# Second chunk's gathers of angles on two semaphores, each waiting for the landing of the one two places ahead

## The chip, the cores and the metric

The kernel runs on one core of a Trainium2 chip. The core has five engines with instruction streams of their own: TensorE (PE in the profile), VectorE (DVE), ScalarE (ACT), GpSimd (POOL) and SyncE (SP). They meet through semaphores, and they share 16 DMA engines. The metric is the device time of one launch in microseconds; the runs of the kernel before took 378.64, 381.76 and 385.66 us, median 381.76.

## The reference, cut to what matters

4,096 token ids (8 batches of 512) each pick a row of 36 angles out of a table of 8,000 rows. The angles drive a simulated circuit of six qubits; its six expectation values, times a matrix and plus a bias, are the embedding of 192 features. A layer norm and an attention over the 512 tokens of a batch follow, then another layer norm and a mixture of eight experts of which each token uses two.

```python
params = quantum_params[token_ids.reshape(-1)]        # 4096 rows of 36 angles
ev = _circuit_expvals(params)                         # sin and cos of half angles, 6 numbers per token
emb = ev @ post_w.T + post_b
h = emb
h = h + attention(layernorm(h))                       # 8 batches of 512 tokens
h = h + top2_of_8_experts(layernorm(h))
```

## The kernel before, in words

Tokens are laid out 128 to a tile, one per partition, so there are 32 tiles of four to a batch. The circuit is computed for two chunks of 16 tiles each (`CHUNK_BATCHES = (4, 4)`). Everything here happens in the first fifth of the run.

**POOL** (`gpsimd` block) sets up an identity, waits for the token ids and then issues 32 indirect DMAs, one per tile, each gathering 128 rows of 36 angles from DRAM into `theta_all` (`gather_angles`, line 421). Each adds 16 to a semaphore when it has landed: the first 16 to that of chunk 0, the others to that of chunk 1. None of them waits for another. Behind them on the same engine stand `constants` (lines 556 to 571), the reciprocal root of chunk 0's variance (`rstd1`, line 540), the pair strings of the second chunk's circuit (`pair_strings(1)`), and later the scatters of rows to experts (line 551) and the final scatter-adds into the output (line 593).

**DVE** (`vector` block) works through a list written out by hand: preparations of weights; `reduce_angles(0)` (lines 655 to 665), which waits until all of chunk 0's angles have landed; copies of weight products; the circuit of chunk 0 in the parts `rotations` (682 to 690), `matrices` (720 to 750), `strings`, `pairs`, `sums`; then `reduce_angles(1)` with its wait for chunk 1's angles; the rest of chunk 0's circuit (`expectations`) and its weights and variance; then the circuit of chunk 1, whose pairs are on POOL. ACT takes sine and cosine of each chunk as soon as the angles are reduced. The attention of chunk 0's batches starts once DVE has written `w` (line 1038), at which PE's transposes (line 1470) wait. Instructions of one part of the circuit stand on DVE in order; `cjoin` waits for those before.

SP loads the small weights and the experts' up weights at the start; the padding of the routing table and the down weights come only when DVE has finished chunk 0's circuit.

Of the kernel before, what the change touches and what calls it, by code (L numbers as in the profile page):

```python
# [30 lines left out]
def build(nc, token_ids, angles, emb_two, emb_raw, qkv_w, gate_w, up_w, down_w, out):  # L31
# [16 lines left out]
    STEPS = -(-BLOCKS // STEP)  # L48
    ROWS = E * REGION + 2 * STEP * P
    RING = 4  # L50
    RESULTS = 8
    CHUNKS = len(CHUNK_BATCHES)
    LAST = [sum(CHUNK_BATCHES[:c + 1]) for c in range(CHUNKS)]
    TILE0 = [(LAST[c] - CHUNK_BATCHES[c]) * TILES for c in range(CHUNKS)]
# [18 lines left out]
    with ctx:  # L73
# [3 lines left out]
        def sem(name):  # L77
            return ctx.enter_context(nc.semaphore(name))
# [88 lines left out]
        def behind(room, pattern, **sizes):  # L167
            size = int(np.prod(list(sizes.values())))
            room[1] += size
            return room[0][:, room[1] - size:room[1]].rearrange(pattern, **sizes)  # L170
# [54 lines left out]

        xb = behind(up_room_1, "p (r n f) -> p r n f", r=RING, n=STEP, f=F)
        y = behind(up_room_1, "p (n d) -> p n d", n=RESULTS, d=D)
        t_own = behind(up_room_1, "p (m x) -> p m x", m=BLOCKS, x=1)
# [8 lines left out]
        bank_d = ctx.enter_context(nc.psum_tensor("bank_d", [P, 512], F32))  # L237

        ids_in = sem("ids_in")
        angles_in = [sem(f"angles_in{c}") for c in range(CHUNKS)]  # L240
        small_in = sem("small_in")
        up_in = sem("up_in")
        down_in = sem("down_in")
# [73 lines left out]
        order_done = sem("order_done")  # L317
        block_in = [sem(f"block_in{r}") for r in range(RING)]
        pick_done = sem("pick_done")
# [7 lines left out]
        y_done = sem("y_done")  # L327
        added = [sem(f"added{n}") for n in range(RESULTS)]
        landed = sem("landed")
# [28 lines left out]
        def _(sp):  # L358
# [23 lines left out]
            def load_block(m):  # L382
                row = sp.value_load(t_i[0:1, 0, m:m + 1], min_val=0, max_val=ROWS - P)
                sp.dma_start(xb[:, m // STEP % RING, m % STEP, :], routed[bass.ds(row, P), :]
                             ).then_inc(block_in[m // STEP % RING], 16)

            sp.sem_inc(landed, 1)
            sp.wait_ge(scattered, 16 * 2 * T)
            sp.wait_ge(table_done, 1)
            for m in range(RING * STEP):  # L390
                if m >= STEP or m % 2 == 0:
                    load_block(m)
            for m in range(BLOCKS):
                sp.wait_ge(added[m % RESULTS], 16 * (m // RESULTS) + 16)
                sp.sem_inc(landed, 1)
                if m + RING * STEP < BLOCKS:
                    load_block(m + RING * STEP)
# [3 lines left out]
        def _(pool):  # L401
# [15 lines left out]
            def gather_angles(first, last):  # L417
                for t in range(first, last):
                    b, j = divmod(t, TILES)
                    c = [b < n for n in LAST].index(True)  # L420
                    pool.indirect_dma_start(out=theta_all[:, t, :], out_offset=None, in_=angles,  # L421
                                            in_offset=bass.IndirectOffsetOnAxis(ids[:, b, j:j + 1], 0)
                                            ).then_inc(angles_in[c], 16)

            step(pool.memset(minus_half[:, :], -0.5))
            pool.wait_ge(ids_in, 16)
            gather_angles(0, T)

            psteps = [0]
# [158 lines left out]
            for m in range(BLOCKS):  # L588
# [6 lines left out]
                        xb[:, m // STEP % RING, m % STEP, DEST:DEST + 1].bitcast(I32), 0),  # L595
                    in_=y[:, m % RESULTS, :], in_offset=None, bounds_check=TOKENS - 1,
                    oob_is_err=False, compute_op=ALU.add).then_inc(added[m % RESULTS], 16)

        @block.vector
        def _(dve):  # L600
# [41 lines left out]
            def cstep(instruction):  # L642
                csteps[0] += 1
                instruction.then_inc(circuit_step, 1)

            def cjoin():
                dve.wait_ge(circuit_step, csteps[0])

            def reduce_angles(c):

                n = COUNT[c]
                theta = theta_all[:, TILE0[c]:TILE0[c] + n, 0:USED]
                count, near, fold = [a[:, 0:n, 0:USED] for a in (turns, turned, folded)]
                dve.wait_ge(angles_in[c], 16 * n)
                cstep(dve.tensor_scalar(count, theta, 1 / (2 * math.pi), ROUNDER, ALU.mult, ALU.add))
                cjoin()
                cstep(dve.tensor_scalar(count, count, ROUNDER, None, ALU.subtract))
                cjoin()
                cstep(dve.scalar_tensor_tensor(theta, count, -TWO_PI_HIGH, theta, ALU.mult, ALU.add))
                cjoin()  # L660
                cstep(dve.scalar_tensor_tensor(theta, count, -TWO_PI_LOW, theta, ALU.mult, ALU.add))
                cjoin()
                dve.tensor_scalar(near, theta, PI_BELOW, -PI_BELOW, ALU.min, ALU.max).then_inc(reduced, 1)  # L663
                dve.wait_ge(reduced, c + 1)
                dve.scalar_tensor_tensor(fold, near, -1.0, near, ALU.mult, ALU.max).then_inc(folded_done, 1)
# [273 lines left out]
            def both_ends(c):  # L939
# [41 lines left out]
            dve.tensor_tensor(form_d[0:E, 0, :, :], bank_b[0:E, 0, 0:E].unsqueeze(2).to_broadcast([E, E, E]), delta,  # L981
                              ALU.mult).then_inc(score_spread, 1)
            reduce_angles(0)
            dve.wait_ge(m2t_done, 1)

# [140 lines left out]
            for part in circuit_parts[0:5]:  # L1126
                part(0)
            reduce_angles(1)
            expectations(0)
            weights()  # L1130
# [51 lines left out]
            c = 0  # L1182
            for shift in (1, 2, 4):
# [3 lines left out]
                c = 1 - c  # L1187
# [57 lines left out]
            def weighted(m):  # L1245
                dve.wait_ge(y_mm, m + 1)
                if m >= RESULTS:
                    dve.wait_ge(added[m % RESULTS], 16 * (m // RESULTS))
# [462 lines left out]
```

## Time and profile before

| what | value |
|---|---|
| runs | 378.64, 381.76, 385.66 us; median 381.76 |
| the profiled execution | 382.33 us, of which the span from first to last instruction is 380.6 |
| busy time over the span | PE 234.4, DVE 171.6, ACT 94.3, POOL 244.9 us |
| gathers of angles (line 421) | 32, from 3.4 to 44.9 us of the span, 32.1 us busy |
| DMA traffic while they run alone | a tenth of the 16 engines' time |

The profile gives for each engine its instructions with start and duration from the span's start, the idle time before them and what seems to have ended it. "issue" is idle time for which the profile shows no releaser. For an indirect DMA the row has the time that POOL worked on issuing it, not the transfer; transfers show in the DMA rows.

### The profile page before, as it was taken

How to read it: one execution, taken by the hardware profiler on the slowest of the kernel's cores; microseconds unless marked ns; L12 is line 12 of the kernel's file. 1: busy time of each engine (PE TensorE's matmuls, PEld its weight loads, DVE VectorE, ACT ScalarE, POOL GpSimd, SP SyncE). 2: the span in 40 equal slices, each digit the busy share in tenths (PEclk: the TensorE clock that was granted, in tenths of full speed). 3: DMA queues.
4: the chain of work that ended last, by engine and by line, in shares of the span. 5: the costliest groups of instructions: out<-in, count | busy, mean ns of one | idle time of the engine just before them, and what ended most of it. 6: DMA issues, size and time to landing. Idle time of an engine off the chain costs nothing. (4 is left out here: it accounts for less than half of the span.)

```text
span 380.6 us, 6129 instructions
## 1 busy us (share of the span) xinstructions
PE 234.4 (62%) x1590; PEld 158.5 (42%) x1590; DVE 171.6 (45%) x649; ACT 94.3 (25%) x221; POOL 244.9 (64%) x259
## 2 busy tenths in 40 slices
PE   1724930067744867673462438999999948999700
PEld 0513510023422434442231215777777726777500
DVE  5836299987466675553153274232232111322200
ACT  1002002015331344440321312342424312333100
POOL 6777700499332657777367751888888388888864
PEclk9999985555685796766555558999999996999955
DMA  7510100890000010110111111655555255555520
GB/s 217 134 16 13 14 1 0 344 373 2 0 0 2 12 52 10 55 51 13 48 48 54 59 47 20 65 65 63 63 62 58 26 58 62 63 65 58 55 27 0
DMA packets 28141, 22.61 MB, mean 59 GB/s; under 512 B 15434, under 2 KB 25546, under 8 KB 27787
## 3 DMA queue, kind: packets, MB, share of 16 engines
q0 software_dynamic: 13296, 7.95, 18.7%
q1 hardware_dynamic: 14524, 14.23, 11.7%
q8 instruction: 15, 0.25, 0.3%
q14 instruction: 18, 0.15, 0.1%
q10 hardware_dynamic: 288, 0.03, 0.1%
HBM read 7.25 MB, written 15.63 MB: 60 GB/s over the span
## 5 line engine op out<-in xcount | busy, mean ns | idle before, releaser
L593 POOL DMA_INDIRECT out<-up x71 | 110.3, 1554 | 40.8 <-DVE up L1249 15.7
L1640 PE MATMUL bank_b<-down,up 128*128 x426 | 87.5, 342 | 5.2 <-issue 1.5
L551 POOL DMA_INDIRECT routed<-rows,slot x64 | 62.3, 973 | 37.0 <-issue 23.1
L1640 PEld LDWEIGHTS bank_b<-down,up 128*128 128x128 f32 x426 | 69.5, 192 | 22.9 <-issue 18.9
L1249 DVE TENSOR_SCALAR up<-bank_b,up 128x192 f32<-128x192 f32 x71 | 29.7, 418 | 96.7 <-PE bank_b L1640 69.2
L421 POOL DMA_INDIRECT theta_all<-angles,ids x32 | 32.1, 1003 | 11.1 <-issue 9.4
L1381 ACT ACTIVATE up<-bank_a 128x384 f32<-128x384 f32 x71 | 31.3, 497 | 2.8 <-PE bank_a L1630 2.4
L540 POOL TENSOR_TENSOR rs<-ve,minus_half 128x16 f32<-128x16 f32 x2 | 7.4, 3711 | 36.8 <-DVE ve L1026 36.8
L1497 PE MATMUL bank_b<-queries_t,keys_t 32*128 32x512 f32 x64 | 24.3, 841 | 7.9 <-DVE nmax L1043 3.0
L1504 PE MATMUL bank_a<-keys_t,wt 32*128 32x512 f32 x64 | 26.1, 898 | 3.4 <-ACT keys_t L1276 2.0
L1570 PE MATMUL bank_a<-m,a2t 32*128 32x192 f32 x64 | 13.6, 510 | 22.7 <-ACT hres L1306 12.1
L1043 DVE TENSOR_REDUCE nmax<-bank_a 128x2 f32<-128x1024 f32 x16 | 19.5, 1219 | 16.3 <-PE bank_a L1504 16.3
L1393 ACT COPY up<-bank_c 128x384 f32<-128x384 f32 x18 | 8.6, 478 | 63.0 <-PE bank_c L1619 50.7
L1470 PE MATMUL bank_a<-ident,w 128*128 128x128 f32 x8 | 3.1, 388 | 31.2 <-DVE w L1038 27.0
L1619 PE MATMUL bank_c<-up_all,up 128*128 128x384 f32 x36 | 16.3, 536 | 9.7 <-DVE up L1209 9.0
L1298 ACT ACTIVATE prob<-bank_b 128x1024 f32<-128x1024 f32 x16 | 16.4, 1023 | 20.1 <-PE bank_b L1497 18.9
L1570 PEld LDWEIGHTS bank_a<-m,a2t 32*128 32x128 f32 x64 | 7.1, 260 | 29.7 <-issue 23.1
L1630 PE MATMUL bank_a<-up 32*128 32x128 f32 x426 | 17.8, 295 | 0.4 <-ACT up L1387 0.4
L1264 ACT ACTIVATE sine<-angle_stages 128x480 f32<-128x480 f32 x2 | 2.1, 1063 | 60.3 <-DVE angle_stages L663 60.3
L1630 PEld LDWEIGHTS bank_a<-up 32*128 32x128 f32 x426 | 14.5, 193 | 4.9 <-issue 4.4
L1470 PEld LDWEIGHTS bank_a<-ident,w 128*128 128x128 f32 x8 | 1.5, 184 | 35.1 <-issue 35.1
L1516 PE MATMUL bank_c<-prob,u 128*32 128x128 f32 x256 | 13.7, 376 | 1.3 <-ACT prob L1298 1.0
(396 smaller groups left out, 373.5 us busy)
## 6 DMA issues: line engine op xcount, KB each, us to landing
routed<-pad_rows SPq DMA_DIRECT2D x8, 528.0 KB, 5.0
out<-hres SPq DMA_DIRECT2D x8, 384.0 KB
down<-down_w SPq DMA_DIRECT2D x1, 2304.0 KB, 9.7
up<-up_w SPq DMA_DIRECT2D x1, 1536.0 KB
out<-up POOLq DMA_INDIRECT x71, 3.5
up<-routed SPq DMA_DIRECT2D x69, 16.0 KB
routed<-rows,slot POOLq DMA_INDIRECT x64
up<-up_w SPq DMA_DIRECT2D x1, 780.0 KB
```

The lines of the kernel that those rows point to most:

```text
L421: pool.indirect_dma_start(out=theta_all[:, t, :], out_offset=None, in_=angles, in_offset=bass.IndirectOffsetOnAxis(ids[:, b, j:j + 1], 0)) ...
L551: pool.indirect_dma_start(out=routed, out_offset=bass.IndirectOffsetOnAxis(slot[:, b, k, j:j + 1], 0), in_=rows[:, b, k, j, :], in_offset= ...
L593: pool.indirect_dma_start(out=out_rows, out_offset=bass.IndirectOffsetOnAxis(xb[:, m // STEP % RING, m % STEP, DEST:DEST + 1].bitcast(I32) ...
L1043: dve.tensor_reduce(nmax[:, b % 2, 2 * h:2 * h + 2], bank_a[:, 0:2, :], AX.X, ALU.max, negate=True).then_inc(max_done, 1)
L1249: dve.tensor_scalar(y[:, m % RESULTS, :], bank_b[:, m % 2, 0:D], xb[:, m // STEP % RING, m % STEP, SHARE:SHARE + 1], None, ALU.mult).then_ ...
L1298: act.activation(prob[:, 2 * h:2 * h + 2, :], bank_b[:, :, :], ACT.Exp).then_inc(exp_done, 1)
L1381: act.activation(hid[:, n, :], bank_a[:, n, 0:HID], ACT.Gelu).then_inc(gelu_done, 1)
L1497: mm = pe.matmul(bank_b[:, n, :], keys_t[r, bt % 3, k * P:(k + 1) * P], queries_t[r, :], start=True, stop=True)
L1504: mm = pe.matmul(bank_a[:, n, :], wt[r, bs % 2, :], keys_t[r, bs % 3, :], start=True, stop=True)
L1570: mm = pe.matmul(bank_a[:, 2 + n, 0:D], a2t[r, :], m2[r, :], start=True, stop=True)
L1630: mm = pe.matmul(bank_a[:, n, c * P:(c + 1) * P], up_now[r, s % 2, c * P:(c + 1) * P], xt[r, 0, :], start=True, stop=True)
L1640: mm = pe.matmul(bank_b[:, m % 2, 0:D], hid[:, m % STEP, c * P:(c + 1) * P], down[:, bass.ds(first + c * D, D)], start=(c == 0), stop=(c = ...
```

## The change

A constant `IN_FLIGHT = 2` is added. Each chunk gets two semaphores in place of one, and its gathers add to them in turn. In the second chunk (c > 0), a gather from the third on first waits until its semaphore has 16 for each earlier gather of the same turn, that is, until the gather two places ahead has landed: 14 waits in all. The first chunk's 16 gathers still wait for nothing. `reduce_angles` waits for both semaphores of its chunk, 128 each, where it waited for one at 256.

```diff
+    IN_FLIGHT = 2
...
-        angles_in = [sem(f"angles_in{c}") for c in range(CHUNKS)]
+        angles_in = [[sem(f"angles_in{c}_{i}") for i in range(IN_FLIGHT)] for c in range(CHUNKS)]
...
                     c = [b < n for n in LAST].index(True)
+                    turn_of, k = divmod(t - TILE0[c], IN_FLIGHT)
+                    if c > 0 and turn_of > 0:
+                        pool.wait_ge(angles_in[c][k], 16 * turn_of)
                     pool.indirect_dma_start(out=theta_all[:, t, :], out_offset=None, in_=angles,
                                             in_offset=bass.IndirectOffsetOnAxis(ids[:, b, j:j + 1], 0)
-                                            ).then_inc(angles_in[c], 16)
+                                            ).then_inc(angles_in[c][k], 16)
...
-                dve.wait_ge(angles_in[c], 16 * n)
+                for k in range(IN_FLIGHT):
+                    dve.wait_ge(angles_in[c][k], 16 * n // IN_FLIGHT)
```

## Rows read from the trace of the kernel before

**Rows 1.** Page, part 1: busy us (share of the span) and instructions of each engine

```profile
PE 234.4 (62%) x1590; PEld 158.5 (42%) x1590; DVE 171.6 (45%) x649; ACT 94.3 (25%) x221; POOL 244.9 (64%) x259
```

**Rows 2.** Timeline of DVE: start us, us, line, operation, tiles, shape [idle before]

```profile
35.05 0.25 DVE L690 TENSOR_TENSOR turn<-cosine,sine 128x96 f32<-128x96 f32 x1
36.57 0.42 DVE L720 TENSOR_TENSOR step_m<-cosine,bloch 128x256 f32<-128x256 f32 x1 [1.27 <-DVE turn L690]
...
37.94 0.19 DVE L733 TENSOR_TENSOR parity<-bloch 128x32 f32<-128x32 f32 x1
38.64 0.17 DVE L734 COPY parity<-bloch 128x16 f32<-128x16 f32 x1 [0.51 <-issue]
...
47.74 0.20 DVE L743 COPY pair_e<-bloch 128x64 f32<-128x64 f32 x1 [1.06 <-issue]
48.45 0.31 DVE L744 TENSOR_TENSOR last_r<-turn 128x144 f32<-128x144 f32 x1 [0.52 <-issue]
48.68 0.18 DVE L747 TENSOR_TENSOR last<-turn,bloch 128x32 f32<-128x32 f32 x1
...
61.94 0.40 DVE L655 TENSOR_SCALAR angle_stages<-theta_all 128x480 f32<-128x480 f32 x1
```

**Rows 3.** Those who stand still until DVE is done, POOL and PE timelines

```profile
71.35 3.71 POOL L540 TENSOR_TENSOR rs<-ve,minus_half 128x16 f32<-128x16 f32 x1 [24.75 <-DVE ve L1026]
77.74 0.45 PE L1470 MATMUL bank_a<-ident,w 128*128 128x128 f32 x1 [26.98 <-DVE w L1038]
```

**Rows 4.** Windows: stretch, us, busy PE, PEld, DVE, ACT, POOL, clock, DMA, GB/s

```profile
36.50:38.00 1.50, 1.50 (x4) 0.97 (x4) 1.43 (x8) 0.00 (x0) 1.20 (x2) 1.00 0.08 12
38.00:48.40 10.40, 10.40 (x25) 5.66 (x24) 2.23 (x11) 0.00 (x0) 7.00 (x15) 1.00 0.10 13
48.40:61.90 13.50, 2.36 (x8) 1.07 (x6) 13.13 (x70) 0.00 (x0) 0.00 (x0) 0.70 0.00 0
```

**Rows 5.** Timeline of POOL, gathers of angles and what follows them

```profile
3.38 1.18 POOL L421 DMA_INDIRECT theta_all<-angles,ids  x1 [1.67 <-DMA ids<-token_ids]
...
34.24 1.89 POOL L421 DMA_INDIRECT theta_all<-angles,ids  x1 [0.30 <-issue]
...
42.72 0.95 POOL L421 DMA_INDIRECT theta_all<-angles,ids  x1 [0.30 <-issue]
43.98 0.95 POOL L421 DMA_INDIRECT theta_all<-angles,ids  x1 [0.30 <-issue]
44.94 0.22 POOL L556 IOTA blk_i<- 128x71 int32 x1
...
46.32 0.28 POOL L569 CAST before<-before_f 128x128 bf16<-128x128 f32 x1
```

**Rows 6.** DMA, 43.98 to 47.98 us in 40 slices of 0.1 us: busy tenths, GB/s

```profile
DMA  0000630000000000552000000000000000000000
GB/s 0 0 0 12 92 69 0 12 0 0 0 0 0 0 0 0 69 81 35 0 0 0 0 0 0 0 0 0 0 0 0 0 0 0 0 0 0 0 0 0
```

**Rows 7.** Timeline of SP and page, part 6: the load of the ids, last number to landing

```profile
0.81 0.46 SPq L359 DMA_DIRECT2D ids<-token_ids  x1
...
ids<-token_ids SPq DMA_DIRECT2D x1, 16.0 KB, 2.3
```

**Rows 8.** Line 593's indirect DMAs, which stand behind waits: timeline, and issue to landing

```profile
259.36 1.55 POOL L593 DMA_INDIRECT out<-up  x1 [0.30 <-issue]
261.22 1.55 POOL L593 DMA_INDIRECT out<-up  x1 [0.30 <-DVE up L1249]
...
DMA to landing us min/median/max: 2.7/3.5/5.1
```

**Rows 9.** DMA, 45.0 to 48.4 us in 40 slices of 0.085 us, and its queues

```profile
DMA  0000000653000000000000000000000000000300
...
q0 software_dynamic: 32, 0.02, 4.0%
q14 instruction: 1, 0.01, 0.9%
```

## The prediction

> **What bounds the kernel now.** I start with the page's busy times: DVE is busy 45% of the span and POOL 64% [rows 1], so no engine is full on average, and the question is what the first 80 us hang on. Then I read DVE's timeline. From 35 us on it runs the circuit of chunk 0, and everybody else stands behind it: POOL's next work after the constants sits idle for 24.75 us until DVE releases it, and PE waits 26.98 us for DVE's `w` before the attention can start [rows 3]. So a microsecond won or lost on DVE between 35 and 77 us moves the rest of the kernel by as much, and a microsecond on POOL in that time moves nothing unless DVE comes to wait for it.
>
> The next thing to see is a slow stretch on DVE. After line 690 it stands 1.27 us, runs normally for eight instructions, and from 37.94 on it starts one instruction every 0.7 or 1.4 us although each takes 0.2 to 0.4 [rows 2]. The table of stretches sums it: of the 10.40 us from 38.0 to 48.4 DVE is busy 2.23, where the stretches before and after it fill 1.43 of 1.50 and 13.13 of 13.50 [rows 4]. That is 10.40 - 2.23 = 8.17 us of idle time, and with the 1.27 in front 9.4 us, all "issue" or a join without a late partner. At 48.45 it is over. The gathers of angles end on POOL at 44.93 and have landed by 46.08 [rows 5, 6]; then the DMA engines are quiet until one packet of the instruction queue at about 48.2 [rows 9], and DVE is back at full speed a quarter of a microsecond later. This is the only place where a change of gathers could touch the time.
>
> **The change part by part.** *The 14 waits on POOL.* A gather starts every 0.95 + 0.30 = 1.26 us (42.72, 43.98) [rows 5]. Gather k now waits for k-2, which started 2 x 1.257 = 2.51 us earlier. When did that land? The last gather starts at 43.98; its packets lie in the slices 16 to 20 of 0.1 us behind that, so it has landed after at most 2.1 us [rows 6]. What does a start cost once the semaphore is there? The first gather waits for the ids, issued at 0.81 and landed 2.3 later, at 3.11 [rows 7], and starts at 3.38: 0.27 us. So gather k may start 2.1 + 0.27 = 2.37 us after k-2 and would have started at 2.51 anyway: the wait is covered with 0.14 us to spare. A wait that is fulfilled costs nothing that one can see: line 593's DMAs stand behind waits too and follow each other with the same 0.30 us [rows 8]. One of the gathers took 1.89 instead of 0.95 [rows 5]; its landing is late by as much, and so is its successor's start, so the margin stays. The lower bound of the 14 waits is 0. Two upper bounds: the first gather, which really waited, took 1.18 instead of 0.95 [rows 5], which makes 14 x 0.23 = 3.2 us; and if landings were to take the 3.5 us of line 593's [rows 8], two gathers would take 3.5 + 0.27 = 3.77 instead of 2.51, which makes 14 x 0.63 = 8.8 us. I take 0, since the gathers' own packets are the nearest row, and keep 8.8 for the range.
>
> The Trainium skill would have it otherwise. "DMA: Bandwidth & Descriptors", in "Anatomy of one DMA — SWDGE (gpsimd) path", gives about 2.0 us fixed per such DMA. Put behind the 0.95 us of issuing, that is 2.95 to landing, 3.22 with the start, and 14 x 0.36 = 5 us as an estimate; by that rule the waits bite. The packets speak against it: 2.1 us with the issuing included [rows 6].
>
> *What is queued behind them on POOL.* `constants` runs from 44.94 to 46.60 [rows 5], and POOL's next work is released by DVE at 71.35, 24.75 us later [rows 3]. 3.2 or 8.8 us of delay both vanish in that. *Who waits for the gathers.* Only DVE's line 655, at 61.94 [rows 2]; the landing at 46.08 is 15.9 us ahead of it, 6.5 even if DVE came 9.4 us earlier. Zero on the path.
>
> *The two extra waits on DVE*, one per chunk, on semaphores which, but for the last gather, are long full. I have no row for a single one; a dispatch with no work in it can hardly be more than the 0.30 us between two gathers [rows 5], nor less than 0. I take 0.1 for the two, and 0.6 as the bound.
>
> *The slow stretch on DVE.* The change doesn't name it. If it has to do with the gathers, as its end suggests, then what matters is how many are under way: before, a gather lives 2.1 us and one starts every 1.26, so two at the most. The limit of two that the change sets is what already holds, and the transfers' place in time stays. So I take 0 for this term, and the bounds are -9.4 (the stretch goes) and, per microsecond by which the gathers take longer, +0.79 (8.17 idle of 10.40).
>
> Sum: 0 + 0 + 0.1 + 0 = +0.1 us. Against the profiled execution of 382.33 us that is 382.4; that execution lies 0.6 above the median of 381.76, and I forecast 381.9 for the median. The runs before spread from 378.64 to 385.66, so two medians of three can differ by 2 us without a cause. About 2% (7.6 us) is what a measurement of this kernel can tell from no change.
>
> **Rivals.** *A: the slow stretch goes, faster.* For it: its end fits the end of the gathers and the one instruction packet behind them [rows 9], as if DVE's next instructions could only be fetched once no gather was queued; with a wait in front of each gather POOL no longer has a row of ready ones. The whole is worth 9.4 us: 381.9 - 9.4 = 372.5, 2.5% faster; half of it gives 377, which is within 2%. After it nothing new is late: the angles are there at 46.08 and would be asked for at 52.5. Against it: the waits come fulfilled, so the stream of packets is the same; and the DMA engines are a tenth busy in that stretch [rows 4], so nothing has to queue for bandwidth. The Trainium skill, "Runtime: NRT & Kernel Launch", "Instruction fetch mechanics", says that an engine's sequencer fetches its next block by a DMA queue of its own and that crossing a block is mostly hidden. Here the packet appears, and the crossing isn't hidden if that is what the stretch is; no row shows when the fetch was asked for. Chance 0.25, 0.20 of it over 2%.
>
> *B: the waits bite and lengthen the slow stretch, slower.* If landing takes longer than 2.24 us (2.51 - 0.27), each further microsecond stretches a gather by half of one. The gathers alone hide in POOL's idle time, but if DVE stays slow until they have landed, it loses 0.79 us for each of theirs. With the 3.5 us of line 593 [rows 8] that is 8.8 x 0.79 = 7.0 us: 388.9. It decides over 2% from 7.6 / 0.79 / 14 = 0.69 us per gather, a landing of 3.6 us. For it: the margin of 0.14 us is thin, and a semaphore may come later than the last packet. Against it: the packets of the very gathers in question. Chance 0.13, 0.10 of it over 2%. The skill's fixed 2.0 us, read as above, is a mild form of B with 5 x 0.79 = 4 us, 386, as an estimate; it would still count as no change.
>
> *C: the waits do nothing at all*, because they are always fulfilled: this is the forecast itself, and the trace will tell it by gathers 1.26 us apart.
>
> **The numbers.** The forecast has 0.62: 381.9, and with the spread of runs 379 to 385. A has 0.25 and B 0.13. The range of 8 in 10 takes in the forecast and A and so begins at 372; above it goes to 386.5, the mild B, and leaves out the rest of B. Faster by over 2%: 0.20; slower: 0.10; within: 0.70.
>
> **What would show it.** Right, if in the new trace chunk 2's gathers still start 1.26 us apart, the last ends near 45 us, and DVE's stretch from 38 to 48 still has about 2 us of work in 10. Rival A would show as DVE running line 733 to 744 in a microsecond or two, with `reduce_angles(1)` near 52 us. B would show as gathers over 1.4 us apart and the slow stretch ending later than 48.4. The prediction is wrong if the slow stretch depends on POOL's queue of ready gathers and not on the packets that they send.

## The result, and the profile after

| | us |
|---|---|
| kernel before, 20 runs beside the new one | 381.51 median (376.66 to 385.66) |
| kernel after, 20 runs | 382.36 median (378.56 to 385.47) |
| ratio after / before, 95% interval | 1.0084 (1.0049 to 1.0118): no change by the bound of 2% |
| the profiled execution of after, its span | 382.2, before 380.6 |

The ratio leaves out as disturbed the runs more than 1.5% above the fastest of their kernel, a limit that falls at 382.3 us for before and at 384.2 us for after, so it drops more high runs of before and overstates the difference. The means over all 20 runs are 382.06 us for after and 381.07 for before, 1.0 us apart. Single runs scatter by 2.0 and 2.4 us (standard deviation), so that difference is known to 2 x sqrt(2.0²/20 + 2.4²/20) = 1.4 us: it can't be told from nothing.

The reading goes in the order of the prediction. First POOL's timeline of after: start, duration, tile, and in brackets the idle time before and its releaser. It answers to [rows 5].

```profile
26.53 0.95 POOL L425 DMA_INDIRECT theta_all<-angles,ids  x1 [0.45 <-DMA theta_all<-angles,ids]
27.78 0.95 POOL L425 DMA_INDIRECT theta_all<-angles,ids  x1 [0.30 <-issue]
...
32.62 0.95 POOL L425 DMA_INDIRECT theta_all<-angles,ids  x1 [0.99 <-DMA theta_all<-angles,ids]
...
35.34 0.95 POOL L425 DMA_INDIRECT theta_all<-angles,ids  x1 [0.53 <-issue]
...
40.74 0.95 POOL L425 DMA_INDIRECT theta_all<-angles,ids  x1 [0.46 <-DMA theta_all<-angles,ids]
41.99 0.95 POOL L425 DMA_INDIRECT theta_all<-angles,ids  x1 [0.30 <-DMA theta_all<-angles,ids]
43.39 0.95 POOL L425 DMA_INDIRECT theta_all<-angles,ids  x1 [0.45 <-DMA theta_all<-angles,ids]
44.65 0.95 POOL L425 DMA_INDIRECT theta_all<-angles,ids  x1 [0.30 <-issue]
```

The waits are not free: every other gather of the second chunk, seven in all, has 0.45 to 0.99 us of idle time in front of it where the others have 0.30, and for five of the seven the profile names the landing of a gather as releaser. Beyond 0.30 each, the seven come to 1.91 us (0.15 + 0.31 + 0.69 + 0.23 + 0.22 + 0.16 + 0.15). From 40.74 to 43.39 a pair takes 2.65 us where the forecast had 2.51; that is the shortest of the seven pairs, their mean is 2.80. Still the last gather starts only 0.67 us later than before (44.65 against 43.98), because before had longer single gathers in the second chunk, one of 1.89 us [rows 5] and one of 1.44, where after has none over 1.02.

Then those who stand still until DVE is done, POOL, DVE and PE timelines of after, for [rows 3] and the last line of [rows 2]:

```profile
71.21 3.71 POOL L544 TENSOR_TENSOR rs<-ve,minus_half 128x16 f32<-128x16 f32 x1 [23.94 <-DVE ve L1031]
...
61.81 0.40 DVE L660 TENSOR_SCALAR angle_stages<-theta_all 128x480 f32<-128x480 f32 x1
...
77.60 0.45 PE L1475 MATMUL bank_a<-ident,w 128*128 128x128 f32 x1 [26.51 <-DVE w L1043]
```

POOL's idle time is shorter by 24.75 - 23.94 = 0.81 us, DVE asks for the angles at 61.81 without a wait, and the attention starts at 77.60, 0.14 us earlier than before. The 1.6 us by which the profiled span is longer come after that, where the kernels are the same, and lie within the scatter of single runs.

Third, DVE's timeline of after in the slow stretch, for [rows 2], and the windows, whose columns are the stretch, its length, busy PE, PEld, DVE, ACT, POOL, the clock, DMA share and GB/s, for [rows 4]:

```profile
37.43 0.17 DVE L739 COPY parity<-bloch 128x16 f32<-128x16 f32 x1 [0.41 <-issue]
37.51 0.18 DVE L740 TENSOR_TENSOR tails<-bloch 128x32 f32<-128x32 f32 x1
38.86 0.17 DVE L741 COPY tails<-bloch 128x16 f32<-128x16 f32 x1 [1.16 <-issue]
40.26 0.19 DVE L742 TENSOR_TENSOR first_h<-bloch 128x32 f32<-128x32 f32 x1 [1.23 <-issue]
...
47.32 0.19 DVE L753 TENSOR_TENSOR last<-turn,bloch 128x32 f32<-128x32 f32 x1 [0.88 <-issue]
48.74 0.17 DVE L754 TENSOR_TENSOR last<-sine,bloch 128x16 f32<-128x16 f32 x1 [1.23 <-issue]
48.84 0.17 DVE L755 TENSOR_TENSOR last<-turn,bloch 128x16 f32<-128x16 f32 x1
```

```profile
36.80:48.80 12.00, 12.00 (x26) 6.47 (x26) 2.40 (x16) 0.00 (x0) 8.04 (x16) 1.00 0.10 12
48.80:61.80 13.00, 2.29 (x8) 1.00 (x6) 12.69 (x67) 0.00 (x0) 0.00 (x0) 0.74 0.00 1
```

The slow stretch is as it was: it begins at the same COPY of `parity`, 12.00 - 2.40 = 9.6 us of it are idle (before 8.17, and the 1.27 in front, which after has not), and DVE is at full speed again from 48.74 on, some 2 us behind the last landing. The single packet of the instruction queue shows again too, near 48.8.

### The profile page after: what moved, and what is told of

It is laid out like the page before. It is cut to its first block and busy times, and to the rows that moved or that the text cites. A ratio compares the mean times of both kernels' runs of the same rounds, so it can differ in the third digit from the quotient of the medians.

```text
span 382.2 us, 6131 instructions
## 1 busy us (share of the span) xinstructions
PE 236.0 (62%) x1590; PEld 159.4 (42%) x1590; DVE 170.9 (45%) x649; ACT 94.4 (25%) x221; POOL 243.6 (64%) x259
## 5 line engine op out<-in xcount | busy, mean ns | idle before, releaser
L425 POOL DMA_INDIRECT theta_all<-angles,ids x32 | 30.8, 963 | 13.1 <-issue 8.1
L1303 ACT ACTIVATE prob<-bank_b 128x1024 f32<-128x1024 f32 x16 | 16.4, 1024 | 22.0 <-PE bank_b L1502 19.3
```

The lines of the kernel that those rows point to most:

```text
L1303: act.activation(prob[:, 2 * h:2 * h + 2, :], bank_b[:, :, :], ACT.Exp).then_inc(exp_done, 1)
```

## The experiments

The runs were made on four chips, and that became part of the result. On the first two the kernel before took 356.5 us, and none of the eight profiles taken there has the slow stretch; on the last two it took 380.8 and 383.1, like the comparison above. Before itself was timed on all four, but its only profile is that of the comparison, so whether it has the stretch elsewhere is read from profiles of its variants and from its time.

### Chips where before takes 356.5 us

**The semaphores without the waits**, run on both chips:

```diff
-                    if c > 0 and turn_of > 0:
-                        pool.wait_ge(angles_in[c][k], 16 * turn_of)
```

> The changed kernel without its 14 waits: the two semaphores a chunk and DVE's extra wait stay. Theory W (the waits cost: a gather that waits starts 0.59 us after the landing it waits for, which makes a pair of gathers 2.66 us and more instead of 2.51, and DVE's slow stretch ends about 2 us after the last landing): gathers 1.26 us apart again, slow stretch as in the kernel before, time within 0.2% of it. Rival S (the second semaphore and DVE's extra wait cost): ratio to before stays near 1.008 and gathers are 1.26 apart all the same. Rival N (nothing but noise): ratio 1.000 here and nothing follows from it for the waits.

> The changed kernel without its 14 waits, again, for the case that DVE has its slow stretch here. Then theory W': gathers 1.26 us apart, slow stretch ends some 2 us behind the last landing as before, ratio 1.000. Rival S: ratio as that of the changed kernel, 1.008. Without the slow stretch both say 1.000.

Measured 0.9992 (0.9974 to 1.001) and 0.9998 (0.9982 to 1.0014) of before. POOL's timeline of the first, at the end of the gathers, which wait for nothing:

```profile
42.44 1.57 POOL L423 DMA_INDIRECT theta_all<-angles,ids  x1 [0.30 <-issue]
44.32 0.95 POOL L423 DMA_INDIRECT theta_all<-angles,ids  x1 [0.30 <-issue]
```

All come after 0.30 us, but single ones take up to 1.57, so the last starts at 44.32 without any wait. The two added waits on DVE cost nothing that these intervals can see (0.2%, 0.7 us).

**The change again**, unaltered:

> The changed kernel as it is, again. In the four runs before this one the kernel before took 356.5 us and DVE ran lines 720 to 744 without a stop; in the traces of the comparison it took 381.5 and DVE had its slow stretch. Theory W' (the waits stretch the gathers by 0.15 us a pair everywhere, but that reaches the time only where DVE has the slow stretch, because only there DVE hangs on the gathers' end): ratio 1.000 within 0.2% if DVE has no slow stretch in this profile, near 1.008 if it has. Rival S (the second semaphore costs time by itself): ratio near 1.008 with or without the slow stretch.

Measured 356.49 against 356.51, ratio 0.9999 (0.9979 to 1.002). It is the cleanest number on the change: nothing, within 0.2%. The waits bite here as well: for 13 of the 14 the profile names a landing as releaser, with up to 1.05 us of idle time. DVE's timeline of this run over the instructions of the slow stretch, then POOL's last gather and PE's start:

```profile
32.71 0.16 DVE L739 COPY parity<-bloch 128x16 f32<-128x16 f32 x1
...
34.11 0.16 DVE L755 TENSOR_TENSOR last<-turn,bloch 128x16 f32<-128x16 f32 x1
```

```profile
44.44 0.95 POOL L425 DMA_INDIRECT theta_all<-angles,ids  x1 [0.30 <-DMA theta_all<-angles,ids]
...
63.52 0.45 PE L1475 MATMUL bank_a<-ident,w 128*128 128x128 f32 x1 [18.79 <-DVE w L1043]
```

From `parity` to the last `last` DVE needs 34.11 - 32.71 = 1.4 us where the profile of after in the comparison took 48.84 - 37.43 = 11.4, with the same gathers running beside it. PE starts the attention at 63.52 in place of 77.60. On this chip the cover is thin: the last gather lands 2.4 us after its start, at 46.8, and DVE asks at 47.7. And here is the packet on which rival A leaned, in the DMA view of this run (46 to 50 us in 40 slices of 0.1, and the queue's line):

```profile
DMA  1760000000000000000000000000020000000000
...
q14 instruction: 1, 0.01, 0.7%
```

It comes at 48.9 although DVE has had no slow stretch to end. It follows POOL's progress, not DVE's: it stands 3.3 us behind the end of the last gather in before (48.2 and 44.93), and again with one in flight below, where that end is 65.1 and the packet comes at 68.4.

**Four in flight**, `IN_FLIGHT = 4`:

> The changed kernel with IN_FLIGHT = 4: four semaphores, 12 waits, each for the landing four places ahead. A gather starts 3 x 1.26 = 3.77 us after the one it then could wait for has started plus one more period, 5.03 in all, and 2.1 + 0.59 = 2.7 is needed, so no wait holds anything. Theory W: gathers 1.26 us apart, ratio to before 1.000, at most 1.002. Rival S (semaphores and extra waits on DVE, now six more): ratio above 1.008. If a wait costs by being there, fulfilled or not, the gathers are further apart than 1.26.

Measured 0.9996 (0.9976 to 1.0015). POOL's timeline, at the last gather:

```profile
43.42 1.17 POOL L425 DMA_INDIRECT theta_all<-angles,ids  x1 [0.31 <-issue]
```

The gathers follow each other after 0.30 us again, and no landing is named as releaser. At a depth of four the waits come fulfilled; at two half of them don't.

**One in flight**, `IN_FLIGHT = 1`, on both chips:

> The changed kernel with IN_FLIGHT = 1: one semaphore a chunk, 15 waits, each for the landing just ahead. Theory W: gathers 2.1 + 0.59 = 2.7 us apart, so the last starts near 65 us and lands near 67; if DVE's slow stretch (one instruction each 0.7 us) lasts until 2 us behind the last landing, it takes in over 60 instructions and reduce_angles(1) starts near 69 instead of 62, later still if DVE's backlog is larger than that: 8 us or more, ratio 1.02 to 1.06. Rival F (the slow stretch has a fixed length of some 12 us whatever the gathers do): DVE is fast again from 48.5, and then waits for the angles until 67, 5 us late: ratio 1.013. Rival P (it needs gathers in a dense row): fewer under way end the slow stretch early and only the angles are late, 5 us.

> Each gather of the second chunk waits for the landing just ahead, again, for the case that DVE has its slow stretch. Last landing near 67 us. Theory W' (slow until 2 us behind the last landing): the slow stretch goes on to near 69 us, DVE's chunk 0 circuit is late by 20 us, time 20 us or more above before where it was 19 without the slow stretch. Rival F (the slow stretch has its own length, 10 to 12 us): DVE is at full speed from 49 us on, and the angles' landing at 67 is what is left to wait for: 5 to 6 us.

Measured 1.056 (1.052 to 1.0601) and 1.0523 (1.049 to 1.0555): 19.3 us more in the second. The first expectation's range of 1.02 to 1.06 holds it by luck, since it was reckoned from a slow stretch that these chips don't show. POOL, DVE and PE timelines of the second, and then its DMA view from the start of the last gather on, in 40 slices of 0.1 us, with the issue's median time to landing:

```profile
61.51 0.95 POOL L425 DMA_INDIRECT theta_all<-angles,ids  x1 [1.65 <-DMA theta_all<-angles,ids]
64.17 0.95 POOL L425 DMA_INDIRECT theta_all<-angles,ids  x1 [1.71 <-DMA theta_all<-angles,ids]
...
66.58 0.48 DVE L660 TENSOR_SCALAR angle_stages<-theta_all 128x480 f32<-128x480 f32 x1 [19.25 <-DMA theta_all<-angles,ids]
...
82.47 0.44 PE L1475 MATMUL bank_a<-ident,w 128*128 128x128 f32 x1 [37.96 <-DVE w L1043]
```

```profile
DMA  0000000000000000392000000000000000000000
...
theta_all<-angles,ids POOLq DMA_INDIRECT x1, 2.4
```

One gather behind the other takes 64.17 - 61.51 = 2.66 us from start to start (2.60 to 2.84 over the 15, 2.69 in the mean). The view splits it: the gather's last packets lie in the slice that ends 1.9 us after its start, but its landing, which is when its semaphore is full, comes at 2.4. So 2.66 - 2.4 = 0.26 us are left for the start behind it. DVE now stands 19.25 us for the angles, PE starts 82.47 - 63.52 = 18.95 us later, and the kernel takes 19.3 more: once the cover is gone, the gathers pass through one for one.

**A pause in the gathers of the kernel before**, after 24 of 32, until DVE has done the first part of chunk 0's circuit:

```diff
-            gather_angles(0, T)
+            gather_angles(0, 24)
+            pool.wait_ge(circuit_step, 38)
+            gather_angles(24, T)
```

> The kernel before with one pause: after 24 of the 32 gathers POOL waits until DVE has done the last instruction of matrices(0) (circuit_step at 38), then issues the other 8. Theory W's part on DVE (DVE's slow stretch ends 2 us behind a landing with nothing after it): the 24th gather lands near 35, DVE becomes slow at most until 37 to 39 us, runs matrices and strings at full speed, and the 8 gathers are issued from about 39 to 49 and have landed by 51, before DVE asks near 53: 7 to 8.5 us won, ratio 0.978 to 0.982. Rival F (fixed stretch of 12 us or a fixed count of slow instructions): DVE stays slow until 48, POOL resumes only then, the angles land near 60: no gain, ratio 1.00. Rival G (DVE is slowed whenever gathers run, not only once): the slowness comes back with the last 8 gathers, gain of 2 us or less.

> POOL waits after 24 gathers until DVE has done matrices(0), again, for the case that DVE has its slow stretch. Theory W': the stretch ends near 39 us, some 8 us won, ratio 0.98. Rival F: DVE stays slow until 48, POOL resumes then, angles land near 60, ratio 1.00 or a little above. Without the slow stretch: 1.000 as before.

Measured 1.0001 (0.998 to 1.0022) and 0.9986 (0.9967 to 1.0004). It says nothing about the slow stretch, since there was none: DVE had counted 38 before POOL was through its 24 gathers, and the pause was no pause (POOL idle for the usual 0.30 us).

### Chips where before takes 381 us

**Waits in both chunks**, 28 in place of 14:

```diff
-                    if c > 0 and turn_of > 0:
+                    if turn_of > 0:
```

> The changed kernel with the waits in the first chunk as well (28 waits): what the wait costs where DVE does stand and wait for the gathers. Theory W (a waiting gather starts 0.59 us after the landing it waits for): the first gathers land late, 4 to 6 us after their start, while the weights are still loading, so about 2.5 us are lost there, and each later pair takes 2.7 instead of 2.51; chunk 0's last landing moves from 24.6 to about 30 us, DVE's reduce_angles(0) with it, and the time by 5 to 5.5 us: ratio 1.014 to 1.016 if DVE has no slow stretch. Rival (the waits are free, as the second chunk's ratio of 1.000 says at face value): ratio below 1.004.

It took 378.9 us (10 runs, 369.49 to 382.29) where before took 380.79 (13 runs, 378.38 to 385.56); the ratio by the rule above is 0.9733 (0.9648 to 0.9818), but it rests on the two lowest of the ten runs, and the result counts as unclear. The means over all runs are 377.64 and 381.31, 3.7 us apart and known to 2.9. It was expected to be slower and isn't. POOL's and DVE's timelines of this run, and then its window:

```profile
12.60 0.95 POOL L425 DMA_INDIRECT theta_all<-angles,ids  x1 [4.53 <-DMA theta_all<-angles,ids]
...
32.65 0.41 DVE L660 TENSOR_SCALAR angle_stages<-theta_all 128x480 f32<-128x480 f32 x1 [10.74 <-DMA theta_all<-angles,ids]
...
40.47 0.33 DVE L739 COPY parity<-bloch 128x16 f32<-128x16 f32 x1
...
41.87 0.16 DVE L755 TENSOR_TENSOR last<-turn,bloch 128x16 f32<-128x16 f32 x1
...
48.80 0.43 DVE L703 TENSOR_TENSOR chain_q<-chain,step_m 128x256 f32<-128x256 f32 x1 [2.33 <-remote]
...
53.05 0.43 DVE L712 TENSOR_TENSOR chain<-chain_q 128x256 f32<-128x256 f32 x1 [2.43 <-remote]
```

```profile
40.40:42.00 1.60, 1.60 (x4) 0.84 (x3) 1.60 (x16) 0.00 (x0) 1.23 (x2) 1.00 0.10 13
```

The delay is there: the first gathers queue up behind landings, by as much as 4.53 us, and DVE stands 10.74 us for chunk 0's angles. But the slow stretch is gone: DVE goes from `parity` to `last` in 1.4 us, with POOL gathering and the DMA engines a tenth busy, as they were in [rows 4]. In the profile of before the last `last` stands here:

```profile
48.97 0.17 DVE L750 TENSOR_TENSOR last<-turn,bloch 128x16 f32<-128x16 f32 x1
```

DVE is not free of unexplained waits, though: it passes the last `last` 7.1 us earlier than before (41.87 against 48.97), and then, with gathers still under way until 52.9, stands 2.33 and 2.43 us for a releaser that the profile calls remote. PE starts at 76.25, only 1.5 us earlier than before.

**Fewer gathers.** The kernel before without the gathers of the last eight tiles; those get the first 1,024 rows of the table by one plain load, for which DVE waits too, so their angles are not those that the ids name:

```diff
+            sp.dma_start(theta_all[:, T - 8:T, :], angles[0:8 * P, :].rearrange("(p n) f -> p n f", n=8)
+                         ).then_inc(plain_in, 16)
...
-            gather_angles(0, T)
+            gather_angles(0, T - 8)
...
```

> The kernel before with 24 gathers instead of 32: the last 8 tiles get their angles by one plain load of the table's first rows instead of by token id, so these tiles' output is not the reference's. The last indirect landing is near 36 us instead of 46. If DVE has its slow stretch here: theory W' (it lasts until 2 us behind the last landing) says it is over near 38 us and 7 to 8 us are won, 0.98; rival F (its own length) says no change. If it has none: DVE asks for the angles at 47.7 anyway, ratio 1.000 within 0.3%, and the instruction queue's packet that stood at 48.2 to 48.9 comes near 39 us, since POOL reaches its next block of instructions earlier; if that packet is DVE's own, it stays where it is.

Measured 373.84 us (4 runs, 370.29 to 376.42), all below the lowest of before, 378.38; the ratio by the rule above is 0.9781 (0.9677 to 0.9886) and counts as unclear. The gathers are over at 33.5, before the circuit, and from DVE's timeline the stretch is gone; another kind of wait is not:

```profile
30.29 0.21 DVE L987 TENSOR_TENSOR form_d<-bank_b,ident 8x64 f32<-8x64 f32 x1 [6.30 <-remote]
...
39.59 0.17 DVE L740 COPY parity<-bloch 128x16 f32<-128x16 f32 x1
...
40.97 0.17 DVE L756 TENSOR_TENSOR last<-turn,bloch 128x16 f32<-128x16 f32 x1
```

**DVE's instructions shifted by 24.** The kernel before with 24 memsets of one column at about 5 us, to see whether the stretch begins at a place in DVE's instruction stream:

```diff
+        spare = sb("spare", [P, 24])
...
+            for i in range(24):
+                step(dve.memset(spare[:, i:i + 1], 0.0))
```

> The kernel before with 24 one-column memsets more on DVE at about 5 us, while it waits for weights. Nothing else moves. Theory I (the slow stretch begins where DVE goes over to its next block of instructions): if DVE has the stretch here, it begins 24 instructions earlier in the program, near line 630 to 990, instead of at line 734. Rival T (it begins at a time or at the same kind of instruction): it begins at line 734 again. If DVE has no slow stretch: the packet of the instruction queue at 26 to 28 us comes earlier by the time of 24 instructions if it is DVE's, and stays if it is another engine's; time unchanged.

One run, 379.76 us, which says nothing on the time. DVE's timeline:

```profile
36.81 0.17 DVE L737 COPY parity<-bloch 128x16 f32<-128x16 f32 x1 [1.21 <-issue]
...
48.01 0.20 DVE L746 COPY pair_e<-bloch 128x64 f32<-128x64 f32 x1 [1.17 <-issue]
```

It begins at the same COPY of `parity`, not 24 instructions earlier. In this profile a boundary in DVE's own instructions is not what starts it. It also shows that this chip, on which the two experiments before were run, has the stretch.

**The pause once more**, on a chip where before takes 383 us:

> Of the kernel before, with the second chunk's gathers stopped after 24 of 32 until DVE has counted 38 steps of its circuit, and then let run. The theory that DVE is slowed by gathers running beside its circuit, on chips where before takes 381 us: the pause comes before the slowed part and the last eight gathers come back beside it, so where DVE reaches step 38 at full speed at least part of the 7.6 us that this part costs above its work is saved, and the ratio is 0.98 to 1.00. The rival, that the slowing depends on where DVE and the gathers stand to each other and not on their number: it can go altogether (0.975) or stay (1.00). On a chip where before takes 356 us and DVE isn't slowed, both expect 1.000, as in the two earlier tries.

Measured 375.05 us (4 runs, 369.68 to 376.40) where before took 383.12 (7 runs, 379.84 to 385.34): 8.1 us or 2.1% less, and no run of the one reaches into the other. No profile of before was taken on this chip, so that it has the stretch here is inferred from its time. POOL's, DVE's and PE's timelines, then two windows:

```profile
32.66 0.95 POOL L421 DMA_INDIRECT theta_all<-angles,ids  x1 [0.30 <-issue]
39.79 1.01 POOL L421 DMA_INDIRECT theta_all<-angles,ids  x1 [6.17 <-DVE last L752]
...
36.53 0.42 DVE L722 TENSOR_TENSOR step_m<-cosine,bloch 128x256 f32<-128x256 f32 x1 [4.71 <-remote]
...
37.98 0.17 DVE L736 COPY parity<-bloch 128x16 f32<-128x16 f32 x1
...
39.35 0.17 DVE L752 TENSOR_TENSOR last<-turn,bloch 128x16 f32<-128x16 f32 x1
...
68.59 0.45 PE L1472 MATMUL bank_a<-ident,w 128*128 128x128 f32 x1 [22.79 <-DVE w L1040]
```

```profile
37.90:39.50 1.60, 1.60 (x7) 0.93 (x6) 1.60 (x16) 0.00 (x0) 0.00 (x0) 1.00 0.00 0
39.70:50.30 10.60, 6.10 (x19) 3.21 (x17) 10.39 (x55) 0.00 (x0) 8.37 (x8) 0.86 0.11 12
```

POOL stands for 6.17 us, DVE goes through the part in question in 1.4 us, and when the last eight gathers run, DVE stays at full speed: 10.39 of 10.60 us busy, beside the very traffic that filled the slow stretch. The stretch doesn't come back with the gathers. PE starts at 68.59, 9.15 us earlier than in the profile of before. What that comes from can be placed: DVE reaches the COPY of `parity` at nearly the same time (37.98 against 38.64, the wait of 4.71 us included), and is through with `last` 9.6 us earlier (39.35 against 48.97).

## Why the prediction was right, and where it was not

The forecast was +0.1 us and no change; the kernel changed by 0.8 us in the medians (382.36 and 381.51), and by nothing within 0.2% on a chip with less scatter. The outcome didn't hang on the term that was wrong, since POOL had 24.75 us to hide it in. Step by step:

**The 14 waits: right in their effect, mis-sized in one term.** The prediction set landing at 2.1 us and the start behind it at 0.27, 2.37 in all against 2.51 of supply, and called the waits covered. The start is right: 0.26 us in the version with one in flight. The landing is the term that was mis-sized. It was read from the gather's last packet, and the semaphore comes later than that: the packets end at 1.9 us, rounded up to 2.1 in the prediction, and the landing comes at 2.4 (the profile gives 2.3 to 2.6 for the waiting gathers of that version). Landing and start together are thus 2.66, not 2.37, and 2.51 us of supply don't cover them. (The 0.59 us to start in the expectations above are counted from 2.1 as well; counted from the landing, they are 0.26.) In after the waits cost POOL 0.14 us in the shortest pair, 0.29 in the mean and 0.69 at most beyond its idle time of 0.30, 1.91 us in all. The bound of 14 x 0.23 = 3.2 us held. Rival B had named this very way to fail, a landing over 2.24 us because a semaphore may come later than the last packet. What the prediction gave as its sign of the forecast, gathers 1.26 us apart, is not what came, and the forecast's name for itself, rival C (always fulfilled), is wrong too.

The rule of the Trainium skill ("DMA: Bandwidth & Descriptors", "Anatomy of one DMA — SWDGE (gpsimd) path"), about 2.0 us fixed, read as the prediction read it, put landing and start at 3.22 us and the waits at 5 us. The trace disagrees with that reading: landing at 2.4 us and the next start at 2.66, with the 0.95 of issuing in both. It is right in that the waits bite.

**Cover on POOL and ahead of DVE: right.** The 0.67 us by which the last gather started later vanished in 24.75 us of idle time, which became 23.94, and DVE asks 15 us after the last landing. How real that cover is, the version with one in flight shows, by taking it away. Without the slow stretch it is only 0.9 us (46.8 to 47.7); behind that, every microsecond of gathers counts in full (18.95 on PE, 19.3 in the time). The prediction's figure of 6.5 us for that case kept the old stretch's other delays; on the faster chips DVE is there 14 us earlier, not 9.4.

**The two waits on DVE: right**, below what can be measured.

**The slow stretch: right that it stays, for half of the reason.** The transfers' place in time hardly moved, and the stretch stayed. That its size follows the gathers by 0.79 per microsecond was rival B's mechanism. It was not put to the test where it could show: the version with one in flight ran only on chips without the stretch. The one profile that bears on it speaks against it: waits in both chunks make the last gather start over 7 us later (51.91) and the stretch is gone, not longer, though DVE too came later there. So B had its first half right, the waits bite, and its price stands unproven.

**Rival A** did not come about, and it lost its evidence: the instruction packet at 48 us comes also where there is no slow stretch, and the shift by 24 instructions didn't move the stretch's first instruction. Its size was good, though: where the stretch goes, as with the pause, PE starts 9.15 us earlier and the kernel takes 8.1 less, for 9.4 forecast.

**What is shown and what stays open.** Shown: gathers beside DVE's circuit are not enough for the stretch (none with waits in both chunks, none on two of the chips, none beside the last eight gathers after the pause), and holding gathers back while DVE passes the part in question goes with 8.1 us less, without overlap of the runs, and with a profile that lacks it (the pause; 24 gathers point the same way). In the three profiles that have it, it began at the same COPY with gathers under way, and it ended 1.7 to 2.7 us behind the last landing (the last start plus 2.4). Whether it can come without gathers, and what in the chip holds DVE back, is not settled. The profiles with waits in both chunks, with 24 gathers, with the shift and with the pause are one each, so a stretch that comes and goes from run to run can't be excluded for them either; the ten runs with waits in both chunks lie as far apart as 369.49 and 382.29. That after keeps the stretch while the version with waits in both chunks loses it speaks for a matter of where DVE and POOL stand to each other; a sweep of that distance was not run.

## What to carry to other kernels

The price of a wait on a DMA's landing is read from two starts with that wait between them, on the engine that waits, and not from the last packet plus a start: here it was 2.66 us per gather, and a depth of two left 0.14 to 0.77 us of a pair uncovered. Nor is the last packet the landing: half a microsecond lay between them. Before costing such a wait, look how long its last consumer is away (15 us on one chip, 0.9 us on another), since behind that it counts one for one. And a stretch in which an engine works a fifth of the time without a releaser is worth an experiment of its own: the pause, an edit of three lines, brought 2.1% on a chip where before takes 383 us, and nothing, but no loss either, where it takes 356.5.

## What the hardware showed that was not expected

- **Chips differ by more than most edits.** The same kernel takes 356.5 us on two chips and 381 to 383 on the others, and 14.1 of the profiled 26.7 us of span (382.2 against 355.5) are there before the attention starts (77.60 against 63.52).
- **Part of it are waits without a visible releaser.** The waits of after on the slower chip (engine, line of the waiting instruction, releaser, us in total, times, longest) have these, put down to "remote", of which the faster chip has none. There the same `form_d` stands for 0.30 us, and the releaser is PE; here it stands for 5.0 ("remote" only says that the profile found nobody; the kernel runs on one core):

```profile
ACT context_t L1307 <- remote: 10.5, 1, 10.5
...
DVE rinv L1061 <- remote: 6.1, 2, 3.8
...
DVE form_d L986 <- remote: 5.0, 1, 5.0
```

- **The profiles of the slower chips lack many semaphore events.** The profile gives a time to landing for the gathers of all eight runs on the faster chips (2.4 us median with one in flight), and for those of none of the six on the slower ones. That fits the many releasers that it can't name there. Whether the recording itself has a part in the slow stretch or in the longer times was not tried.
- **In the slow stretch DVE starts keep a beat of 1.40 or 0.70 us.** In before each start from 38.64 to 48.45 is 0.70 or 1.40 us behind the last; in after waits end 1.40 us apart (38.86, 40.26, 41.69, 43.09, 44.52, 45.92), and at some a second instruction follows at once. It is not the gathers' 1.26 us, and PE's granted clock is 1.00 meanwhile, the level of 2.4 GHz.
- **Single gathers take longer without a wait in sight**: up to 1.57 and 1.89 us for one of 0.95. The number in flight doesn't explain it: in the first version with one in flight one took 1.54, and in the version with 24 memsets, which bounds nothing, none of the second chunk over 1.09. By such differences 14 waits that cost 1.91 us moved the last gather by only 0.67.
